# Expert weights split into parts in the front through three buffers, and the last shared outputs stored from ACT's queue

## The chip, the cores and the metric

The kernel runs on one core of one Trainium2 chip. The metric is the device time of one execution in microseconds. In the profile PE is TensorE, PEld its weight loads, DVE is VectorE, ACT ScalarE, POOL GpSimd and SP SyncE; SPq, ACTq and POOLq are the DMA issues of an engine. DVE runs everything that subtracts and adds, ACT what copies, scales or applies a function, SP only issues DMAs and waits.

## The reference

X is (2, 2048, 512) in fp32, so 4096 tokens of width D = 512; H = 256 per expert, E = 8 experts, two for each token.

```python
h = layernorm(layernorm(X)) * ln_w + ln_b
Q, K, V = split(h @ W_in + b_in); Q, K = rope(Q), rope(K)
A = sum over tokens of (K / |K|) * V          # one vector per sequence
x2 = X + layernorm((A * Q) @ W_out + b_out + layernorm(X))
xf = layernorm(x2)
top_logits, idx = top_k(xf @ gate_w, 2); gates = softmax(top_logits)
routed = sum over the two experts of gate * (gelu(xf @ w1[e] + b1[e]) @ w2[e] + b2[e])
shared = gelu(xf @ sw1 + sb1) @ sw2 + sb2
out = x2 + layernorm(routed + shared)
```

## The kernel before

Each fp32 factor is held as a high and a low part, and each product is three matmuls (hi·hi, lo·hi, hi·lo; lines 1434 to 1436). ACT makes the high part by a copy, DVE (in a few places POOL) the low part by a subtraction. Tokens go in NG = 8 groups of G = 512, a group in GT = 4 tiles of 128. Each engine has its own program, and the order in it is written out by hand; semaphores tie them together.

**Front** (span 26 to 316 us). For each group g: K and V products of four tiles (`kv`), the turn of the next group's h (`turn`, eight transposes a bank in two banks of `tp`, for which ACT writes `hb` and the high part in `front_split(g+1)`), then the Q products (`q`). DVE does `k_tile`, `v_tile` and `kv_prod` of a tile, `q_lo_parts(g-1)` after the third tile's K, and `rotate_q(g)`; ACT does `norm_k(g, j)`, the square of a K tile, for which it waits on DVE, and after the fourth `front_split(g+1)` and `bias_q(g)`. SP issues, in this order in each group: `load_x(g+2)`, `store_q(g-1)` (waits for `q_lo_parts(g-1)`), `load_rt(g+1)`, `load_rf(g+1)`, and then, in g = 1 to 4, copies of two experts' `w1` and `w2` from DRAM to `expert_scratch`, laid out anew, and in g = 5 those of `sw1` and `sw2`. The output weights `wo` are scaled by A at the ends of the two sequences, `scale_wo(0)` after group GB = 4.

**Attend** (316 to 570). For group s: `attend(s, j)` is A·Q@W_out plus a rank one product with `bo` (64 rows, of which two hold the parts of b_out; L1509), `z_tile`, `x2_tile`, `norm_x2(s)`; between them the normalised n3 of group s-1 is turned (`n3_turn`) and gated (`gate`). A `fill` slot (s = 2 to 7) puts a half of a shared expert of the groups in EARLY there: "h" (first product, `hs`, gelu, low parts) in one s, "o" (second product, `f_out`, stores of f) in the next. At s = 0 ACT and POOL split the shared weights (`split_s`); load order on SP is q, s. The experts' weights are 64 KB a partition in `we[e]`: parts 2i (high) and 2i+1 (raw, then low). After the last group SP loads raw parts (`load_expert`), ACT makes `split_expert`, DVE `expert_lo`.

**Routing** (566 to 657). `n3_turn(7)`, `shared_o(6, j)`, `gate(7)`, counts and ranks of the experts (`rank_ps`), `shared_h(7, m)`, then 16 blocks of the hot loop (L1601: DVE makes marks `hot_a`, `hot_q` for HT tiles, ACT scales `hot_a`, PE multiplies them into the list of token ids), with `shared_o(7, j)` and `f_out(7, j)` between them; then POOL gathers rows by indirect DMA.

**Expert loop** (657 to 910). NRT = 72 tiles of 128 slots: gather, turn, `h_of`, gelu, `o_of`, gate, and scatter with addition to `f_scratch`, which was zeroed for the groups in LATE and holds the shared outputs for those in EARLY.

**Late** (910 to 1026). For the three groups of LATE: `late_turn` (two banks `tp`, `nc_hi` by ACT, `nc_lo` by DVE), `late_h`, `late_o`; and for all groups `normed`, the layer norm of f, whose result POOL adds to `out` in DRAM by accumulating stores (L1413). Its weights `c1`, `c2` are loaded raw and split there again. `measured` and `normed_in` say after which late product each early tile's moments and norm stand.

Of the kernel before, what the change touches and what calls it, by code (L numbers as in the profile page):

```python
# [7 lines left out]
P = 128  # L8
F32 = mybir.dt.float32
# [4 lines left out]
ALU = mybir.AluOpType  # L14
# [5 lines left out]
EARLY = (1, 3, 5, 6, 7)  # L20


def sandwich_kernel(nc, X, ln_w, ln_b, W_in, b_in, W_out, b_out, gate_w, w1, b1, w2, b2,
# [39 lines left out]
    we_dram = dram("expert_scratch", (E, 2, P, KD * H))  # L63
    ws_dram = dram("shared_scratch", (2, P, KD * SH))
# [9 lines left out]
    with ctx:  # L74
# [23 lines left out]
        upper, ones_f = keep("upper", [P, P]), keep("ones_f", [P, P])  # L98
# [43 lines left out]
        wo_lo = [at("wo_lo0", 136, [P, KD, D], F32R), at("wo_lo1", 8, [P, KD, D], F32R)]  # L142
        rc, rsn = at("rc", 144, [P, 2, G]), at("rsn", 148, [P, 2, G])
# [3 lines left out]
        sq, prod = [at(f"sq{i}", 176 + 2 * i, [P, D]) for i in range(2)], [at(f"prod{i}", 180 + 2 * i, [P, D]) for i in range(2)]  # L147
# [3 lines left out]
        raw_o = [at(f"raw_o{i}", kb_, [P, D]) for i, kb_ in enumerate((194, 196, 198, 110))]  # L151
# [8 lines left out]
        bo_raw, bo_hi = at("bo_raw", 96, [B_ROWS, D]), at("bo_hi", 98, [B_ROWS, D], F32R)  # L160
        bo, bo_one = at("bo", 108, [B_ROWS, D], F32R), at("bo_one", 100, [B_ROWS, P], F32R)
# [11 lines left out]
        zero_d = at("zero_d", 72, [P, D])  # L173
# [32 lines left out]
        c1_hi, c1_lo = at("c1_hi", 96, [P, KD, SH], F32R), at("c1_lo", 104, [P, KD, SH], F32R)  # L206
        c2_hi, c2_lo = at("c2_hi", 112, [P, KS, D], F32R), at("c2_lo", 120, [P, KS, D], F32R)
        c_raw = [at(f"c_raw{i}", kb_, [P, KD, SH]) for i, kb_ in enumerate((136, 164))]
        hsc = [at(f"hsc{i}", 144 + 2 * i, [P, G]) for i in range(2)]
        hc_hi, hc_lo = at("hc_hi", 148, [P, KS, G], F32R), at("hc_lo", 156, [P, KS, G], F32R)  # L210
        fst, fmv = at("fst", 192.125, [P, NT, 6]), at("fmv", 193, [P, NT, 2])
# [7 lines left out]
        rank_ps, ids_ps = bank[2], bank[0]  # L219
        xt_ps, th_ps, h_ps, oe_ps = bank[0:2], (bank[2], bank[7]), bank[3:5], bank[5:7]  # L220
# [9 lines left out]

        fill = {2 + i: (("h", "o")[i % 2], EARLY[i // 2]) for i in range(6)}
        assert all(fill[s][1] == s - 1 for s in (2, 4, 6))
# [8 lines left out]
        h_order = (1, 3, 5, 6, 7)  # L241
# [3 lines left out]
        f_buf = {n: n % 2 for n in range(len(f_order) - GT)}  # L245
        f_buf.update({len(f_order) - GT + j: (2, 3, 4, 0)[j] for j in range(GT)})
        f_buf_uses = [sum(b == u for b in f_buf.values()) for u in range(2)] + [3]

        def f_sem(u):
            return f_stored[min(u, 2)]  # L250
# [14 lines left out]
        measured = beside((0, 0, 0, 0, 1, 1, 1, 1, 2, 2, 2, 2, 1, 1, 0, 0, 2, 2, 1, 1, 0, 0, 0, 0))  # L265
        normed_in = beside((0, 0, 0, 0, 0, 0, 0, 0, 0, 1, 1, 1, 2, 2, 2, 2, 1, 1, 1, 1, 2, 1, 1, 1))
# [16 lines left out]
        f_loads = (EARLY[0], LATE[0], EARLY[1], EARLY[2], LATE[1], EARLY[3], LATE[2], EARLY[4])  # L283


        w_order = (3, 4, 0, 5, 1, 2, 6, 7)

        front_in, consts_in, late_in, rows_in = sem("front_in"), sem("consts_in"), sem("late_in"), sem("rows_in")
# [8 lines left out]
        we_copied, ws_copied = sem("we_copied"), sem("ws_copied")  # L297
# [13 lines left out]
        bo_in, bo_set, bo_hi_done, bo_split = sem("bo_in"), sem("bo_set"), sem("bo_hi_done"), sem("bo_split")  # L311
# [4 lines left out]
        x2_stored, n3_stored, f_stored = [sem(f"x2_stored{i}") for i in range(2)], sem("n3_stored"), [sem(f"f_stored{i}") for i in range(3)]  # L316
# [3 lines left out]
        s_in, s_hi_done, s_split = [sem(f"s_in{i}") for i in range(2)], sem("s_hi_done"), sem("s_split")  # L320
# [6 lines left out]
        we_in, we_hi_done, we_split = [sem(f"we_in{i}") for i in range(E)], sem("we_hi_done"), sem("we_split")  # L327
        bias_in = [sem(f"bias_in{i}") for i in range(2)]
# [9 lines left out]
        c_split = sem("c_split")  # L338
        n3c_in, f_in = [sem(f"n3c_in{i}") for i in range(len(LATE))], [sem(f"f_in{i}") for i in range(NG // 2)]
# [4 lines left out]
        y_normed, stored = sem("y_normed"), sem("stored")  # L344
# [4 lines left out]
        def _(sp):  # L349
# [29 lines left out]
            sp.dma_start(b2_rows[:, :], b2).then_inc(rows_in, 16)  # L379
            sp.dma_start(sb2_rows[:, :], sb2.partition_broadcast(E)).then_inc(rows_in, 16)  # L380
# [3 lines left out]
            for k in range(KD):  # L384
                sp.dma_start(raw_o[k][:, :], W_out[k * P:(k + 1) * P, :]).then_inc(o_raw_in, 16)
# [3 lines left out]
            def copy_expert(e):  # L389
                sp.dma_start(we_dram[e, 0].rearrange("p (k h) -> p k h", k=KD), w1[e].rearrange("(k p) h -> p k h", p=P))\  # L390
                  .then_inc(we_copied, 16)
                sp.dma_start(we_dram[e, 1].rearrange("p (k d) -> p k d", k=KH), w2[e].rearrange("(k p) d -> p k d", p=P))\
                  .then_inc(we_copied, 16)
# [5 lines left out]

            for g in range(NG):  # L400
# [12 lines left out]
                if g == 5:  # L413
                    for i, w in enumerate((sw1, sw2)):
                        sp.dma_start(ws_dram[i].rearrange("p (k h) -> p k h", k=KD), w.rearrange("(k p) h -> p k h", p=P))\
                          .then_inc(ws_copied, 16)
# [6 lines left out]
            def load_s(i, lo):  # L423
                sp.dma_start(lo[:, :, :].rearrange("p k h -> p (k h)").bitcast(F32), ws_dram[i]).then_inc(s_in[i], 16)

            sp.wait_ge(tp_full, KD * NG)
            sp.dma_start(bo_raw[:, :], b_out.partition_broadcast(B_ROWS)).then_inc(bo_in, 16)
# [16 lines left out]
            for s in range(NG):  # L444
# [3 lines left out]
                if s == 2:  # L448
                    sp.wait_ge(consts_set, F_ZERO)
                    for g in LATE:  # L450
                        sp.dma_start(f_groups[g], zero_d[:, :].rearrange("p (o d) -> p o d", o=1).to_broadcast([P, GT, D]))\
                          .then_inc(zero_stored, 16)
                    sp.dma_start(f_dram[N:N + 4 * P, :].rearrange("(t p) d -> p t d", p=P),
                                 zero_d[:, :].rearrange("p (o d) -> p o d", o=1).to_broadcast([P, 4, D])).then_inc(zero_stored, 16)
# [6 lines left out]
                if s + 2 < NG:  # L461
                    load_x(NG + s + 2)
# [1304 lines left out]
```

## Time and profile before

| | us |
|---|---|
| median of 3 runs (lowest, highest) | 1025.62 (1023.91, 1026.31) |
| profiled execution, own time | 1027.98 |
| its span | 1025.8 |
| TensorE busy in the span | 896.8 |
| VectorE busy | 628.3 |
| ScalarE busy | 442.0 |
| GpSimd busy | 404.4 |
| mean granted TensorE clock | 0.95 |

The span is the part that the profiler records; 2.2 us of the execution's own time lie outside it. Busy time is the time in which an engine works on some instruction; waiting for semaphores and issuing DMAs is not in it. The granted clock is 1.00 at TensorE's higher level (2.4 GHz) and 0.50 at its lower one (1.2 GHz); a value between is a mean over a stretch in which both occur. DMA share is the mean busy share of the core's sixteen DMA engines. In a timeline row the bracket at the end is the idle time of the engine before the instruction, and what it had waited for; in the list of waits "times" counts the waits and the last number is the longest.

### The profile page before, as it was taken

Reading aid. Unit: us, or ns where it says so; the run is one execution under the profiler, and the core shown is the slowest. Engines: PE = TensorE matmul, PEld = TensorE weight load, DVE = VectorE, ACT = ScalarE, POOL = GpSimd, SP = SyncE. Lnnn points to the kernel's source line nnn. Section 1 sums busy time; section 2 is a strip of 40 time slices with the busy share of each in tenths; the row PEclk is TensorE's granted clock in tenths of the full one; section 3 lists DMA queues with packets and bytes.
Section 4 is the critical chain, followed back from the end, with each engine's and each line's share of the span. In section 5 each row is a group of like instructions: output and inputs, shape, how many; then the busy total and the mean of one; then the engine's idle time right before and its main releaser. Section 6 shows DMA issues by size and latency. Waiting matters only on the chain.

```text
span 1025.8 us, 14729 instructions
## 1 busy us (share of the span) xinstructions
PE 896.8 (87%) x4562; PEld 739.3 (72%) x4562; DVE 628.3 (61%) x1356; ACT 442.0 (43%) x830; POOL 404.4 (39%) x337
## 2 busy tenths in 40 slices
PE   1999999999997699999999748499999999969883
PEld 1877787787785467777778537488988988857662
DVE  5656766676664775656665587366665666655653
ACT  4134233433423124122242645366666666653462
POOL 3356446545631400000000000277677777730464
PEclk9999999999998889999999878799999999989886
DMA  9122644545337568645424650678778878789496
GB/s 314 45 81 105 244 143 161 188 158 200 135 144 306 190 239 312 227 165 215 154 83 169 215 151 32 238 144 149 140 147 163 154 146 149 147 176 350 62 160 107
DMA packets 78074, 174.68 MB, mean 170 GB/s; under 512 B 10841, under 2 KB 19289, under 8 KB 73137
## 3 DMA queue, kind: packets, MB, share of 16 engines
q1 hardware_dynamic: 52096, 124.60, 33.6%
q0 software_dynamic: 20592, 45.96, 25.1%
q10 hardware_dynamic: 5312, 3.18, 1.3%
q8 instruction: 41, 0.67, 0.3%
q14 instruction: 33, 0.26, 0.1%
HBM read 103.68 MB, written 80.53 MB: 180 GB/s over the span
## 4 chain that ended last, share of the span: by engine, by line
PE 70%; DVE 11%; issue 7%; ACT 4%; POOL 3%; DMA 2%; SPq 1%; POOLq 0%; ACTq 0%; DVEq 0%
PE bank L1434 12%; PE bank L1435 12%; PE bank L1436 12%; PE bank L1626 3%; PE bank L1628 3%; PE bank L1627 3%; PE bank L1643 3%; PE bank L1645 3%; PE bank L1644 3%; PE bank L1613 3%; PE bank L1429 3%; POOL out L1413 2%; DVE we L1061 2%; PE bank L1635 2%; ACT hb L535 1%
## 5 line engine op out<-in xcount | busy, mean ns | idle before, releaser
L1385 POOL DMA_INDIRECT f_scratch<-ro,dst x71 | 113.2, 1595 | 48.7 <-SPq L513 23.2
L1377 POOL DMA_INDIRECT xr<-n_scratch,ids x72 | 71.1, 987 | 90.9 <-issue 65.6
L1434 PE MATMUL bank<-wkv_hi,h_hi 128*128 128x512 f32 x256 | 101.1, 395 | 3.8 <-issue 3.8
L1436 PE MATMUL bank<-wkv_hi,h_lo 128*128 128x512 f32 x256 | 100.7, 393 | 0.0
L1435 PE MATMUL bank<-wkv_lo,h_hi 128*128 128x512 f32 x256 | 100.6, 393 | 0.0
L1188 DVE TENSOR_TENSOR ro<-bank,b2b 128x512 f32<-128x512 f32 x71 | 49.1, 692 | 70.3 <-PE bank L1645 70.3
L1626 PE MATMUL bank<-we,x_hi 128*128 x284 | 86.4, 304 | 0.0
L1628 PE MATMUL bank<-we,x_lo 128*128 x284 | 80.7, 284 | 0.0
L1627 PE MATMUL bank<-we,x_hi 128*128 x284 | 80.6, 284 | 0.0
L544 ACT ACTIVATE sq<-kb 128x512 f32<-128x512 f32 x32 | 20.3, 633 | 134.2 <-DVE kb L845 134.2
L1344 POOL TENSOR_TENSOR zr<-zv,half 128x4 f32<-128x4 f32 x8 | 8.1, 1009 | 137.7 <-DVE zv L961 137.7
L1296 POOL TENSOR_TENSOR rn<-ssq,half 128x1 f32<-128x1 f32 x32 | 23.4, 731 | 96.2 <-ACT sq L544 96.2
L1434 PEld LDWEIGHTS bank<-wkv_hi,h_hi 128*128 128x128 f32 x256 | 48.7, 190 | 14.3 <-issue 4.2
L1643 PE MATMUL bank<-we,g_hi 128*128 x142 | 56.6, 399 | 1.2 <-DVE g_lo L1180 1.2
L1168 DVE TENSOR_TENSOR x_lo<-bank,x_hi 128x512 fp32r<-128x512 f32 x72 | 49.7, 690 | 11.4 <-ACT x_hi L704 9.9
L1645 PE MATMUL bank<-we,g_lo 128*128 x142 | 56.4, 397 | 0.0
L1435 PEld LDWEIGHTS bank<-wkv_lo,h_hi 128*128 128x128 f32 x256 | 48.8, 191 | 10.2
L1644 PE MATMUL bank<-we,g_hi 128*128 x142 | 56.1, 395 | 0.0
L1436 PEld LDWEIGHTS bank<-wkv_hi,h_lo 128*128 128x128 f32 x256 | 48.6, 190 | 10.3
L1626 PEld LDWEIGHTS bank<-we,x_hi 128*128 128x128 f32 x284 | 54.3, 191 | 0.3 <-issue 0.3
L1434 PE MATMUL bank<-wo_hi,q_hi 128*128 128x512 f32 x128 | 54.3, 424 | 0.0
L1627 PEld LDWEIGHTS bank<-we,x_hi 128*128 128x128 f32 x284 | 54.3, 191 | 0.0
(232 smaller groups left out, 2514.2 us busy)
## 6 DMA issues: line engine op xcount, KB each, us to landing
xg<-in_X SPq DMA_DIRECT2D x16, 1024.0 KB, 9.1
q_scratch<-qh SPq DMA_DIRECT2D x8, 1024.0 KB, 3.9
q_scratch<-qb SPq DMA_DIRECT2D x8, 1024.0 KB, 7.1
expert_scratch<-in_w SPq DMA_DIRECT2D x16, 512.0 KB, 7.1
q_hi<-q_scratch SPq DMA_DIRECT2D x8, 1024.0 KB, 4.7
q_lo<-q_scratch SPq DMA_DIRECT2D x8, 1024.0 KB, 6.9
out<-z SPq DMA_DIRECT2D x8, 1024.0 KB, 5.1
n_scratch<-n SPq DMA_DIRECT2D x8, 1024.0 KB, 6.4
```

The source lines that it names most:

```text
L1168: dve.tensor_tensor(x_lo[u][:, :], xt_ps[u][:, :], x_hi[u][:, :].bitcast(F32), ALU.subtract)\
L1377: pool.indirect_dma_start(xr[u][:, :], None, n3_dram, bass.IndirectOffsetOnAxis(ids[:, i:i + 1], 0)).then_inc(row_in[u], 16)
L1385: pool.indirect_dma_start(f_dram, bass.IndirectOffsetOnAxis(dst[:, i:i + 1], 0), ro[i % NRO][:, :], None, compute_op=ALU.add).then_inc(r_s ...
L1434: pe.matmul(dst, hi(k), w_hi(k), start=(k == 0), stop=False)
L1435: pe.matmul(dst, hi(k), w_lo(k), start=False, stop=False)
L1436: last = pe.matmul(dst, lo(k), w_hi(k), start=False, stop=(k == KD - 1 and not more))
L1626: pe.matmul(out_h, x_hi[u][:, s], part_of(e, 0, k, H), start=(k == 0), stop=False)
L1627: pe.matmul(out_h, x_hi[u][:, s], part_of(e, 1, k, H), start=False, stop=False)
L1628: last = pe.matmul(out_h, x_lo[u][:, s], part_of(e, 0, k, H), start=False, stop=(k == KD - 1))
L1643: pe.matmul(oe_ps[u][:, :], g_hi[u][:, s], part_of(e, 2, k, D), start=(k == 0), stop=False)
L1644: pe.matmul(oe_ps[u][:, :], g_hi[u][:, s], part_of(e, 3, k, D), start=False, stop=False)
L1645: last = pe.matmul(oe_ps[u][:, :], g_lo[u][:, s], part_of(e, 2, k, D), start=False, stop=(k == KH - 1))
```

## The change

The order of the groups' shared experts is another one: EARLY is (0, 2, 4, 6, 7), with fill slots s = 1 to 7. Expert and shared weights are no longer copied from DRAM to DRAM and split later. They are 20 units of 512 KB; in each of the groups 1 to 5 four units are loaded to SBUF, split by one ACT copy (`unit_hi`) and one DVE subtraction (`unit_lo`) and stored as two parts, through three pairs of buffers (UB = 3). So `split_s`, `split_expert`, `expert_lo` and the splits of c1 and c2 are gone, and twice as many bytes are loaded for experts (16 MB) and shared weights. The parts of b_out are made in group 0. f of group 6 and 7 is stored from ACT's queue, group 6 through buffers of its own. At s = 7 the DVE does the whole x2 chain at once. Two of the `shared_o(7, j)` come ahead of the hot loop. In the late stage n3 and c1_hi are loaded only after the first eight turns of the expert loop, `late_turn` uses four banks, each f load has its own semaphore, and the last late group is written by plain stores from SP after DVE has added x2.

```diff
-EARLY = (1, 3, 5, 6, 7)
+EARLY = (0, 2, 4, 6, 7)
...
-    we_dram = dram("expert_scratch", (E, 2, P, KD * H))
-    ws_dram = dram("shared_scratch", (2, P, KD * SH))
+    we_dram = dram("expert_scratch", (E, 4, P, KD * H))
+    ws_dram = dram("shared_scratch", (2, 2, P, KD * SH))
...
+        UG = 4
+        units = [(e, i, 0) for e in range(E) for i in range(2)] + [(E + i, 0, h) for i in range(2) for h in range(2)]
+        UB = 3
+        w_lo = [at(f"w_lo{i}", kb_, [P, UW], F32R) for i, kb_ in enumerate((128, 132, 194))]
+        w_hi = [at(f"w_hi{i}", kb_, [P, UW], F32R) for i, kb_ in enumerate((136, 140, 176))]
...
+            def load_unit(u):
+                if u >= len(units):
+                    return
+                if u >= UB:
+                    sp.wait_ge(w_stored[u % UB], 32 * (u // UB))
+                w, k = unit_in(u)
+                sp.dma_start(w_lo[u % UB][:, :].bitcast(F32).rearrange("p (k h) -> p k h", k=k), w).then_inc(raw_w_in[u % UB], 16)
+
+            def store_unit(u):
+                sp.wait_ge(unit_split, u + 1)
+                for c, w in ((0, w_hi), (1, w_lo)):
+                    sp.dma_start(unit_out(u, c), w[u % UB][:, :].bitcast(F32)).then_inc(w_stored[u % UB], 16)
...
             for g in range(NG):
+                u = UG * (g - 1)
+                with_units = 0 <= u < len(units)
                 sp.wait_ge(h_normed, g + 1)
                 load_x(g + 2)
+                if with_units:
+                    store_unit(u)
+                    load_unit(u + 2)
                 if g >= 1:
                     store_q(g - 1)
+                if with_units:
+                    store_unit(u + 1)
+                    load_unit(u + 3)
+                    store_unit(u + 2)
+                    load_unit(u + 4)
                 if g + 1 < NG:
                     sp.wait_ge(k_rotated, GT * (g + 1))
                     load_rt(g + 1)
+                if with_units:
+                    store_unit(u + 3)
+                    load_unit(u + 5)
+                if g + 1 < NG:
                     sp.wait_ge(q_rotated, g + 1)
                     load_rf(g + 1)
-                if 1 <= g <= 4:
-                    copy_expert(2 * g - 2)
-                    copy_expert(2 * g - 1)
...
-            sp.wait_ge(ws_copied, 32)
-            load_s(1, s2_lo)
             store_q(NG - 1)
+            for u in range(UB):
+                sp.wait_ge(w_stored[u], 32 * u_uses[u])
             sp.wait_ge(q_stored[1], 32 * NG // 2)
             load_q(1)
-            load_s(0, s1_lo)
+            load_s(0, (s1_hi, s1_lo))
...
+            def load_expert(e, parts=range(4)):
+                c = slice(parts[0], parts[-1] + 1)
+                sp.dma_start(we[:, e, c, :].bitcast(F32), we_dram[e, c].rearrange("c p h -> p c h")).then_inc(we_in, 16)
...
+            for j in range(GT):
+                sp.wait_ge(y_added, j + 1)
+                sp.dma_start(out_tiles[GT * LATE[2] + j], f[LATE[2]][:, j, :]).then_inc(late_stored, 16)
...
+            def unit_hi(u):
+                act.wait_ge(raw_w_in[u % UB], 16 * (u // UB + 1))
+                if u >= UB:
+                    act.wait_ge(w_stored[u % UB], 32 * (u // UB))
+                act.activation(w_hi[u % UB][:, :], w_lo[u % UB][:, :].bitcast(F32), ACT.Copy).then_inc(unit_hi_done, 1)
...
                     if j == 1 and g >= 1:
                         q_hi_parts(g - 1)
+                    if 0 <= UG * (g - 1) < len(units):
+                        unit_hi(UG * (g - 1) + j)
                 if g + 1 < NG:
                     front_split(g + 1, (g + 1) % 2)
...
-            act.wait_ge(bo_in, 16)
-            act.activation(bo_hi[:, :], bo_raw[:, :], ACT.Copy).then_inc(bo_hi_done, 1)
-            act.wait_ge(bo_set, 1)
-            act.activation(bo[0:1, :], bo_raw[0:1, :], ACT.Copy).then_inc(bo_split, 1)
...
             for m in range(KS):
                 gelu(7, m)
-            split_expert(2)
+                store_f(6, m)
...
             for k in range(KD):
                 act.wait_ge(tc_full, KD * i + k + 1)
-                act.activation(nc_hi[:, k, :], tp[k % 2][:, :], ACT.Copy).then_inc(nc_hi_done, 1)
+                act.activation(nc_hi[:, k, :], tc[k][:, :], ACT.Copy).then_inc(nc_hi_done, 1)
...
                 kv_prod(g, 0)
+                unit_lo(g, 0)
...
                     q_lo_parts(g - 1)
+                unit_lo(g, 1)
...
                 kv_prod(g, 2)
+                unit_lo(g, 2)
                 v_tile(g, 3)
                 kv_prod(g, 3)
+                unit_lo(g, 3)
                 rotate_q(g)
...
-            expert_lo((5, 1, 2, 6))
...
-                if b in (4, 7, 10, 13):
-                    f_out(7, (b - 4) // 3)
-                if b == 9:
-                    expert_lo((7,))
+                for j in {2: (0, 1), 5: (2,), 8: (3,)}.get(b, ()):
+                    f_out(7, j)
...
             for s in range(NG):
                 z_rsqrt(s)
-                if s == 0:
-                    split_s(1, s2_hi, s2_lo)
                 x2_rsqrt(s)
-                if s == 0:
-                    split_s(0, s1_hi, s1_lo)
```

## Rows read from the trace of the kernel before

**Rows 1.** The page's engine totals: busy us, share of the span, instructions.
```profile
PE 896.8 (87%) x4562; PEld 739.3 (72%) x4562; DVE 628.3 (61%) x1356; ACT 442.0 (43%) x830; POOL 404.4 (39%) x337
```

**Rows 2.** Windows by stage: stretch, length, busy us of PE, PEld, DVE, ACT, POOL; clock, DMA share, GB/s.
```profile
100.00:200.00 100.00, 96.51 (x445) 78.99 (x444) 69.09 (x140) 33.90 (x59) 49.06 (x38) 1.00 0.53 188
600.00:640.00 40.00, 22.39 (x106) 18.89 (x104) 33.44 (x60) 22.52 (x66) 0.00 (x0) 0.74 0.28 74
900.00:940.00 40.00, 30.31 (x147) 24.59 (x146) 18.61 (x27) 19.51 (x32) 8.49 (x5) 0.87 0.90 266
980.00:1026.00 46.00, 24.45 (x93) 18.90 (x91) 17.37 (x55) 18.48 (x27) 24.17 (x29) 0.76 0.85 136
```

**Rows 3.** TensorE's waits over the span: us in total, times, longest.
```profile
PE bank L1601 <- ACT hot_a L698: 19.6, 4, 15.5
PE bank L1429 <- DVE n_lo L991: 15.3, 8, 7.2
...
PE bank L1429 <- ACT hb L535: 12.6, 16, 4.3
PE bank L1613 <- DMA xr<-n_scratch,ids: 10.4, 2, 5.9
PE bank L1429 <- DVE nc_lo L1211: 10.4, 3, 4.4
PE bank L1429 <- ACT n L628: 9.9, 1, 9.9
PE bank L1509 <- DVE bo L935: 6.7, 1, 6.7
```

**Rows 4.** Timeline of the front's group 2: start, us, engine, line, operation.
```profile
100.86 0.39 PE L1434 MATMUL bank<-wkv_hi,h_hi 128*128 128x512 f32 x1
...
114.73 0.69 DVE L836 TENSOR_TENSOR kb<-bank,bkv 128x512 f32<-128x512 f32 x1 [0.34 <-PE bank L1436]
...
117.33 2.35 DVE L877 TENSOR_TENSOR qb<-qb,qh 128x1024 f32<-128x1024 f32 x2
...
123.26 0.78 ACT L535 ACTIVATE hb<-bank,lnb,lnw 128x512 f32<-128x512 f32 x1 [0.30 <-PE bank L1429]
...
137.06 0.39 PE L1434 MATMUL bank<-wkv_hi,h_hi 128*128 128x512 f32 x1
```

**Rows 5.** Groups by shape of the experts' splits: busy us, mean ns, idle before.
```profile
L674 ACT ACTIVATE we<-we 128x1024 fp32r<-128x1024 f32 x16 | 15.6, 1043 | 1.5 <-DVE picked L1127 1.5
...
L1061 DVE TENSOR_TENSOR we<-we 128x1024 fp32r<-128x1024 f32 x16 | 18.5, 1219 | 0.0
```

**Rows 6.** Windows: a stretch of the front, and the start of attend.
```profile
120.00:125.00 5.00, 4.32 (x25) 3.32 (x23) 4.83 (x9) 2.37 (x5) 2.62 (x3) 1.00 0.94 367
...
326.00:331.50 5.50, 5.50 (x12) 4.01 (x13) 1.54 (x3) 0.23 (x1) 0.00 (x0) 0.50 0.79 301
```

**Rows 7.** DMA issues from 100 to 137 us: KB each, us to landing.
```profile
q_scratch<-qb SPq DMA_DIRECT2D x1, 1024.0 KB, 7.1
rf<-in_rope_feat SPq DMA_DIRECT2D x1, 512.0 KB, 4.2
```

**Rows 8.** Timeline at the start of attend, and z of the next group.
```profile
326.41 0.43 SPq L420 DMA_DIRECT2D q_lo<-q_scratch  x1
...
342.35 4.73 POOL L1355 TENSOR_TENSOR s_lo<-s_lo,s_hi 128x1024 fp32r<-128x1024 f32 x2
...
344.68 3.61 DVE L967 SCALAR_TENSOR_TENSOR z<-z,zr,xg 128x512 f32<-128x512 f32 x2
...
371.19 1.41 DVE L967 SCALAR_TENSOR_TENSOR z<-z,zr,xg 128x512 f32<-128x512 f32 x2
```

**Rows 9.** The page's DMA issues over the span: KB each, us to landing.
```profile
q_lo<-q_scratch SPq DMA_DIRECT2D x8, 1024.0 KB, 6.9
```

**Rows 10.** Timeline of the routing, DVE.
```profile
591.85 0.69 DVE L1023 COPY fo<-bank 128x512 f32<-128x512 f32 x1 [2.52 <-DMA f_scratch<-fo]
```

**Rows 11.** Timeline of the end, POOL's last stores.
```profile
1011.18 4.44 POOL L1413 DMA_DIRECT2D out<-f  x5
```

More of the change, by code:

```diff
@@ L142, in sandwich_kernel @@
         wo_lo = [at("wo_lo0", 136, [P, KD, D], F32R), at("wo_lo1", 8, [P, KD, D], F32R)]
+        UW = KD * H
+        UG = 4
[3 more added lines that the diff above has]
+        w_hi = [at(f"w_hi{i}", kb_, [P, UW], F32R) for i, kb_ in enumerate((136, 140, 176))]
+        u_uses = [len(range(i, len(units), UB)) for i in range(UB)]
         rc, rsn = at("rc", 144, [P, 2, G]), at("rsn", 148, [P, 2, G])
@@ L599, in _ @@
                     keep_acol(0)
+                if g == GB + 2:
+                    for u in range(UB):
+                        act.wait_ge(w_stored[u], 32 * u_uses[u])
                     scale_wo(0)
@@ L629, in norm_x2 @@
                                    scale=xr_[:, j:j + 1]).then_inc(n3_ready, 1)
-            def split_s(i, hi, lo):
-                act.wait_ge(s_in[i], 16)
-                for h in range(2):
-                    s = slice(2 * h, 2 * h + 2)
-                    act.activation(hi[:, s, :], lo[:, s, :].bitcast(F32), ACT.Copy).then_inc(s_hi_done, 1)
             def gelu(g, m):
@@ L782, in _ @@
                     gelu_c(i, m)
-                for g, j in y_of[what, i, m]:
-                    normed(g, j)
                 if what == "h" and m == KS - 1 and i + 1 < len(LATE):
@@ L787, in _ @@
                         nc_hi_part(i + 1, k)
+                for g, j in y_of[what, i, m]:
+                    normed(g, j)
             normed(*y_order[-1])
@@ L877, in q_lo_parts, with unit_lo @@
                     dve.tensor_tensor(q[:, s, :], q[:, s, :], qh[:, s, :].bitcast(F32), ALU.subtract).then_inc(q_split, 1)
+            def unit_lo(g, j):
+                u = UG * (g - 1) + j
+                if 0 <= u < len(units):
+                    dve.wait_ge(unit_hi_done, u + 1)
+                    dve.tensor_tensor(w_lo[u % UB][:, :], w_lo[u % UB][:, :].bitcast(F32), w_hi[u % UB][:, :].bitcast(F32), ALU.subtract)\
+                       .then_inc(unit_split, 1)
             def wo_lo_parts(b):
-                if b == 0:
-                    dve.wait_ge(b2_stored, 16)
                 for k in range(KD):
@@ L1055, in _ @@
             s = NG - 1
-            def expert_lo(es):
-                for e in es:
-                    for i in range(2):
-                        dve.wait_ge(we_hi_done, 2 * w_order.index(e) + i + 1)
-                        lo = we[:, e, 2 * i + 1, :]
-                        dve.tensor_tensor(lo, lo.bitcast(F32), we[:, e, 2 * i, :].bitcast(F32), ALU.subtract)\
-                           .then_inc(we_split, 1)
-            for m in range(KS):
+            x2_tile(s, 0)
+            x2_tile(s, 1)
+            x2_stats(s, 0)
+            x2_tile(s, 2)
+            x2_stats(s, 1)
+            x2_tile(s, 3)
+            x2_stats(s, 2)
+            x2_stats(s, 3)
+            x2_moments(s)
+            hs_lo_part(6, 0)
+            x2_shift(s)
+            for m in range(1, KS):
                 hs_lo_part(6, m)
+            top2(s - 1)
             dve.memset(zero_q[:, :].bitcast(F32), 0.0)
@@ L1085, in _ @@
             f_out(6, 3)
-            expert_lo((0,))
             dve.wait_ge(counts_full, 1)
@@ L1370, in _ @@
             pool.wait_ge(gates_stored, 16)
-            for u in range(3):
+            pool.wait_ge(zero_stored, 16 * (len(LATE) + 1))
+            for u in range(4):
                 pool.wait_ge(f_stored[u], 16 * f_buf_uses[u])
@@ L1576, in _ @@
                     part(g, i)
-            for m in range(KS):
-                shared_h(6, m)
             n3_turn(NG - 1)
@@ L1590, in _ @@
             pe.matmul(rank_ps[:, 0:E * NT], upper[:, :], marks, start=True, stop=True)
-            pe.matmul(rank_ps[:, E * NT:2 * E * NT], ones_f[:, :], marks, start=True, stop=True).then_inc(counts_full, 1)
+            pe.matmul(rank_ps[:, E * NT:2 * E * NT], ones_f[:, :].bitcast(F32), marks, start=True, stop=True).then_inc(counts_full, 1)
             for m in range(KS):
                 shared_h(7, m)
+            shared_o(7, 0)
+            shared_o(7, 1)
             pe.wait_ge(consts_set, ZEROS_SET)
```

303 lines of the change are left out of this document (156 added, 147 removed).

## Prediction

> **What bounds the kernel now.** I read the engines' totals first: TensorE is busy 87% of the span, every other engine under two thirds [rows 1]. So time is gained or lost where TensorE stands idle or runs at its lower clock, and the windows by stage say where that is. In the front the reader is to see 96.5 us of matmuls in 100 at granted clock 1.00; the ends are elsewhere: in the routing 22 us of 40 at 0.74, at the end of the expert loop 30 of 40 at 0.87, in the last 46 us 24 [rows 2]. The list of TensorE's waits names what it stood for [rows 3]: the marks (19.6 us), `n_lo` (15.3), `nc_lo` (10.4), the first gathers (10.4), n of group 0 (9.9), `bo` (6.7). Of `hb`, the front's own input, it waits only 12.6 us in 16 times: this list is also a list of what has cover and can lose it. Last come the timelines around each edit.
>
> **The front, g = 1..5: the loss.** Call T the start of a group's K products (100.86); the next group's is 36.2 us on [rows 4]. ACT has nothing to do from the last `norm_k` until the banks of the next turn are full, and starts `front_split` at 123.26, T+22.4; TensorE needs it at once (the following turn, then the Q products). The change puts `unit_hi(4g-1)` in that place, and it waits for a DMA. When does that DMA land? SP issues it behind `store_q(g-1)` and `store_unit(4g-3)`. `store_q` waits for `q_lo_parts`, which ends at 119.68, T+18.8. One `unit_lo` is put ahead of it on the DVE, one behind it: 1.22 each [rows 5], of which the DVE's idle 0.34 at 114.73 takes some, so `store_q` is issued at T+19.7. In front of the unit's last byte there are then 2 MiB of Q, 1 MiB of the unit's parts and its own 0.5: 3.67 MB. At the 367 GB/s from 120 to 125 [rows 6] 10.0 us; the row of `q_scratch<-qb` (2 MiB, landed 7.1 us after its issue, of which 5.7 are bytes [rows 7]) adds 1.4, and the issues 0.4. It lands at T+31.5, and ACT's copy, 1.04 [rows 5], ends at T+32.6. That is 10.2 after `front_split` starts now, and TensorE stands for it. Behind the waiting copy on ACT are `front_split` and `bias_q`; on SP, `store_unit(4g-1)` waits for the same unit, and `load_rf(g+1)` behind it has a whole group of time. A stall also lowers the clock: after the 6.7 us wait for `bo` the window from 326 to 331.5 shows 0.50, the lower of its two levels [rows 6], which costs 2.7. I take 2.2 us here, since the first microsecond is transposes that ACT paces anyway. 12.4 a group, five groups: **62**.
> Bounds. If the load doesn't queue behind the stores, it is issued at T+22.2 and lands in the 4.2 us of `rf` (512 KB) [rows 7]: stall 5.0, clock 1.5, together 32.5. If the DMA is in time, ACT's 1.04 and the DVE's added copies ahead of the last K tiles (4 × 1.22 a group, the DVE at 69% [rows 2]) leave about 3.3 a group, 16.5. If the queue is a tenth slower, 68. I take the queue, because the row of `rf` itself (4.2 for 1.4 us of bytes) and `qb` both show landings that grow with what was issued before.
> The Trainium skill (DMA: Bandwidth & Descriptors, section "Anatomy of one DMA — SWDGE (gpsimd) path") gives about 2.0 us fixed and 436 GB/s for a transfer; its fit is for transfers issued by GpSimd, so for these it is an estimate. By it the 3.67 MB would take 10.4 us instead of the rows' 11.4, and the sum would be 5 us lower, 1026; the rows' rate is used.
> The `bo` parts in g = 0 cost ACT 0.3 there, and the stores of `f(0,*)`, now behind the zero fills, about 1.0. Loss **63.3**.
> Covered: the loads' bytes themselves (the queues are at 0.53 in the front [rows 2]), POOL in the front (49%), SP's waits, since nothing SP holds back but `rf` and `rt` is needed within a group.
>
> **Start of attend: a gain.** `bo` is ready long before: 6.7 of wait [rows 3] and 2.7 of half clock go. The wait for n of group 0, 9.9 [rows 3], goes too: POOL's `s_lo` splits, 4.73 for two [rows 8], stretch the DVE's instructions beside them (z for two tiles 3.61, later 1.41 [rows 8]) and delay the chain z, x2, n. Against it `load_q(1)`, issued at 326.41 [rows 8], lands at 333.3 (6.9 us, [rows 9]), when TensorE is ready for it at 329.7: 3.3 for it and 1.0 of clock. Sum **15.0**; bounds 9 (the chain stays) to 19 (no new wait).
>
> **Routing: a gain.** `n_lo` of the last group waits 7.2 [rows 3]; with x2's chain ahead of everything at s = 7 I work out 4.0, so 3.3, and 1.4 earlier in that chain. `f_out(6,*)` gets own buffers, and the 2.52 wait for a store [rows 10] and 0.8 behind it go: 3.3. `expert_lo(5,1,2,6)`, eight of 1.15, 9.2 [rows 5], stands between the gates and the marks, for which TensorE waits; 2.5 come back as waits for `hs`: 6.7. In the hot loop `expert_lo(7)` goes, 2.4, and 1.6 of waits for banks: 4.0. Gathers of the first rows wait behind two other loads; of the 10.4 [rows 3] go 4.1. Less 1.3 for clock. Sum **21.5**, bounds 14 to 27. The cover that this needs: 16 MB of expert parts instead of 8. Counted from the stage in which they start, they and the biases land 8 to 10 us before the expert loop asks.
>
> **Late: a gain.** With four banks and n3 in time the waits for `nc_lo` go, 10.4 [rows 3], and the clock of 0.87 over 40 us [rows 2], 5.2, with it: 16 with what remains of `hc_lo`. After the last matmul five accumulating stores follow one another from POOL, 4.44 for the issue alone [rows 11], to the end at 1025.8; one plain store a tile from SP behind one DVE add saves 5.5 (bounds 2 to 8). **21.5**, bounds 15 to 25.
>
> **Sum.** Gains 15.0 + 21.5 + 21.5 = 58.0, losses 63.3: +5.3. The profiled execution took 1027.98 us (span 1025.8), so 1033.3 for it; the median of the three runs shown is 1025.62, 2.4 below, so **1031**. The two sides are of one size, each with some 8 us of doubt: the sign hangs on the front. Break-even is a loss of 11.3 a group, a landing at T+30.4.
>
> **Rivals.**
> *A, the unit's load passes the stores* (other side). If the sixteen engines serve a later read beside queued writes, the stall is 5.0 and a group loses 6.5: losses 33.8, gains 58.0, **1001**. For it: `rf` landed after 4.2 us. Against it: it was issued when the Q stores had nearly drained. It decides from a landing before T+30.4.
> *B, the expert parts become the wait.* They, b1 and b2, 17.8 MB, take 48.5 us at 367 GB/s; at the 266 GB/s of a shared stretch [rows 2] 67, and 18.5 less the 8 of slack and with the clock after a stall is about 12 more: **1043**. For it: gathers, zero fills and stores of x2 and f share these queues. Against it: the routing's share is 0.28 [rows 2].
> *C, the units are in time*, and only ACT's and DVE's instructions count: losses 17.8, **985**. It needs `store_q` out of the way, for which no row speaks.
>
> **How the numbers follow.** Forecast (values 1020 to 1042) 0.50; A 0.27; B 0.14; C 0.09. Within 0.2% (2 us, what a measurement here can tell from no change) of 1025.62 lies 0.08 of the forecast, faster 0.08, slower 0.34. Faster: 0.08 + 0.27 + 0.09 = 0.44; same 0.08; slower 0.34 + 0.14 = 0.48. The range reaches down into A, whose own values are 996 to 1008, and up over B's middle: 997 to 1048, and leaves out C and the edges. The likeliest case's own range is 1020 to 1042.
>
> **What would show it.** Right: in five groups TensorE waits about 10 us in the turn's transposes on ACT `hb`, ACT being idle before a copy `w_hi<-w_lo` that a DMA releases, at a distance from K products to K products of 48.6, not 36.2; no wait on `bo`; a wait of 3 us for `q_hi` or `q_lo`; the marks' wait under 8; no wait of note for `nc_lo`; 10 us from the last matmul to the end instead of 17. Wrong: a distance of 42.7 (A) or 39.5 (C); the first expert matmul waiting for `we` (B). The forecast falls if the loads land before T+30, or if any of the three gains is under its lower bound.

## The result and the profile after

The changed kernel took 1050.27 us (1046.55 to 1053.11, 4 runs) beside 1024.88 for the kernel before: ratio 1.0244, 95% interval 1.0208 to 1.0281. That is 25 us slower, where 5 us slower was forecast, and 2 us above the top of the range. Its profiled execution took 1049.15 us, span 1047.4, so 21.6 more than the span before. The kernel before took 1025.6 us on one chip and 1030.1 on another (medians), so below a run is compared by its ratio to the kernel before on the same chip, or inside one trace.

Stage by stage, from the first and last start of a group of instructions in the two traces (us from the span's start):

| TensorE at | before | after | difference |
|---|---|---|---|
| last K product of the front | 303.9 | 359.5 | +55.6 |
| first turn of n (group 0) | 359.0 | 402.0 | +43.0 |
| last turn of n (group 7) | 575.6 | 618.9 | +43.3 |
| DVE's first marks of the hot loop | 615.8 | 649.0 | +33.2 |
| last matmul of the hot loop | 644.3 | 682.6 | +38.3 |
| first product of the expert loop | 657.3 | 691.7 | +34.4 |
| first late turn | 911.0 | 947.6 | +36.6 |
| last matmul of all | 1008.2 | 1039.0 | +30.8 |
| end of the span | 1025.8 | 1047.4 | +21.6 |

The loss is in the front, and it never comes back in full. TensorE's waits after, which answer to [rows 3] (us in total, times, longest):

```profile
PE bank L1481 <- ACT hb L598: 58.0, 16, 10.3
...
PE bank L1481 <- DVE n_lo L1046: 10.6, 8, 2.0
PE bank L1655 <- ACT hot_a L751: 9.4, 6, 6.4
PE bank L1667 <- DMA xr<-n_scratch,ids: 5.9, 2, 5.7
PE bank L1481 <- DMA n3c<-n_scratch: 4.8, 1, 4.8
PE bank L1486 <- DVE hc_lo L1276: 4.4, 2, 2.2
...
PE bank L1486 <- DMA q_lo<-q_scratch: 3.8, 1, 3.8
PE bank L1486 <- DVE fo L1080: 3.6, 1, 3.6
...
PE bank L1740 <- DMA c_lo<-shared_scratch: 1.9, 1, 1.9
```

`bo` and `nc_lo` are gone; `hb` has risen from 12.6 to 58.0. The 9.9 us wait for n of group 0 is gone too: its turn, at 401.98, has no wait ahead of it. The 1.5 us that the list still has for `ACT n` stand in the last group:

```profile
612.64 0.66 PE L1481 MATMUL bank<-ident,n 128*128 128x128 f32 x4 [1.55 <-ACT n L702]
```

The timeline of one front group, which answers to [rows 4], shows how:

```profile
111.09 0.39 PE L1486 MATMUL bank<-wkv_hi,h_hi 128*128 128x512 f32 x1
...
130.65 0.32 SPq L426 DMA_DIRECT2D q_scratch<-qh  x1
...
134.53 1.24 SPq L416 DMA_DIRECT2D w_lo<-in_w  x1
...
142.30 1.06 ACT L647 ACTIVATE w_hi<-w_lo 128x1024 fp32r<-128x1024 f32 x1 [6.17 <-DMA w_lo<-in_w]
143.26 0.76 ACT L598 ACTIVATE hb<-bank,lnb,lnw 128x512 f32<-128x512 f32 x1
...
144.07 1.12 PE L1481 MATMUL bank<-ident,hn 128*128 128x128 f32 x4 [10.18 <-ACT hb L598]
...
158.65 0.39 PE L1486 MATMUL bank<-wkv_hi,h_hi 128*128 128x512 f32 x1
```

Read from T = 111.09: Q's stores at T+19.6, the fourth unit's load at T+23.4, its copy at T+31.2, TensorE idle for 10.18 us, and the next group 47.6 us on instead of 36.2.

In the hot loop a new row stands on ACT's queue. Its second number is the time of the issue itself:

```profile
656.99 0.36 ACT L751 ACTIVATE hot_a<-hot_a,token 128x72 fp32r<-128x72 f32 x1 [3.87 <-DVE hot_q L1201]
657.00 7.58 ACTq L740 DMA_DIRECT2D f_scratch<-fo  x1
...
665.11 0.60 ACT L751 ACTIVATE hot_a<-hot_a,token 128x72 fp32r<-128x72 f32 x2 [7.02 <-issue]
```

ACT can't scale the next marks while it stands in that issue, and TensorE waits 6.39 us for them. And near the start of the late stage the windows show TensorE idle for 9 us in 30, with the queues full (length, busy us of PE, PEld, DVE, ACT, POOL, clock, DMA share, GB/s):

```profile
950.00:980.00 30.00, 21.22 (x89) 17.48 (x90) 12.76 (x28) 8.61 (x14) 2.74 (x3) 0.89 0.95 327
980.00:1010.00 30.00, 27.82 (x130) 22.74 (x129) 24.88 (x73) 16.28 (x25) 15.28 (x19) 1.00 0.96 258
```

The kernel before has the same picture in the first 30 us of its late stage, but its queues are emptier behind them, at 136 GB/s:

```profile
910.00:940.00 30.00, 21.60 (x92) 17.44 (x93) 13.26 (x17) 14.12 (x21) 4.60 (x3) 0.83 1.00 329
940.00:970.00 30.00, 25.60 (x111) 21.23 (x110) 22.39 (x63) 14.00 (x21) 11.12 (x13) 0.89 0.62 136
```

### The profile page after: what moved, and what is told of

It is laid out like the page before. It is cut to its first block, busy times and chain, and to the rows that moved or that the text cites. A ratio compares the mean times of both kernels' runs of the same rounds, so it can differ in the third digit from the quotient of the medians.

```text
span 1047.4 us, 14773 instructions
## 1 busy us (share of the span) xinstructions
PE 905.8 (86%) x4562; PEld 746.4 (71%) x4562; DVE 627.1 (60%) x1359; ACT 438.8 (42%) x826; POOL 399.6 (38%) x329
## 4 chain that ended last, share of the span: by engine, by line
PE 60%; DVE 16%; DMA 10%; ACT 6%; issue 5%; SPq 2%; POOL 1%; DVEq 0%; POOLq 0%; ACTq 0%
PE bank L1486 10%; PE bank L1487 9%; PE bank L1488 9%; PE bank L1680 3%; PE bank L1681 3%; PE bank L1682 3%; PE bank L1697 3%; PE bank L1699 3%; PE bank L1698 3%; DMA w_lo<-in_w 3%; PE bank L1667 3%; DMA f_scratch<-ro,dst 2%; PE bank L1481 2%; DVE w_lo L929 2%; PE bank L1689 1%
## 5 line engine op out<-in xcount | busy, mean ns | idle before, releaser
L1481 PE MATMUL bank<-ident,hn 128*128 128x128 f32 x128 | 25.2, 345 | 71.1 <-ACT hb L598 58.0
L1481 PEld LDWEIGHTS bank<-ident,hn 128*128 128x128 f32 x128 | 18.4, 175 | 76.9 <-ACT hb L598 62.9
L1356 POOL TENSOR_TENSOR rn<-ssq,half 128x1 f32<-128x1 f32 x32 | 27.5, 860 | 106.5 <-ACT sq L607 106.5
L1486 PEld LDWEIGHTS bank<-wkv_hi,h_hi 128*128 128x128 f32 x256 | 48.6, 190 | 14.3 <-issue 4.2
L1487 PEld LDWEIGHTS bank<-wkv_lo,h_hi 128*128 128x128 f32 x256 | 48.6, 190 | 10.2
L1488 PEld LDWEIGHTS bank<-wkv_hi,h_lo 128*128 128x128 f32 x256 | 48.6, 190 | 10.2
L702 ACT ACTIVATE n<-z,xnm,xr__76 128x512 f32<-128x512 f32 x32 | 23.5, 805 | 77.2 <-DVE xnm L1039 77.2
```

What stands on the lines that cost most here:

```text
L1481: last = pe.transpose(dst[:, j * P:(j + 1) * P], src[:, j, k * P:(k + 1) * P], ident[:, :])
L1486: pe.matmul(dst, hi(k), w_hi(k), start=(k == 0), stop=False)
L1487: pe.matmul(dst, hi(k), w_lo(k), start=False, stop=False)
L1488: last = pe.matmul(dst, lo(k), w_hi(k), start=False, stop=(k == KD - 1 and not more))
```

## The experiments

Each is an edit of the changed kernel unless it says otherwise.

**The fourth unit off the front's path.**

```diff
-                    if 0 <= UG * (g - 1) < len(units):
+                    if 0 <= UG * (g - 1) < len(units) and j < GT - 1:
                         unit_hi(UG * (g - 1) + j)
                 if g + 1 < NG:
                     front_split(g + 1, (g + 1) % 2)
                     bias_q(g)
+                if 0 <= UG * (g - 1) < len(units):
+                    unit_hi(UG * (g - 1) + GT - 1)
...
-                unit_lo(g, 3)
                 rotate_q(g)
                 if g + 2 < NG:
                     front_stats(g + 2)
+                unit_lo(g, 3)
```

> The changed kernel with the fourth unit of each group taken off the front's path: its ACT copy stands behind front_split and bias_q, its DVE subtraction behind rotate_q. Theory (the fourth unit's load, queued behind the stores, holds ACT and so the turn): the distance from K products to K products falls from 47.6 us to 36.5 to 38.5, TensorE's wait on hb from 58.0 us to under 16, and the time from 1050 to about 1003 (995 to 1012). Rival (the added DVE copies, four of 1.22 us a group, or the doubled bytes bound the group): the distance stays above 42 and the time above 1025.

Ratio 0.9883 (0.9859 to 0.9906): 3.5% less than the changed kernel, some 37 us, and now faster than the kernel before. On the scale of the kernel before, 1025.6 us, that is 1014, just above the expected 995 to 1012. The wait on `hb` is 24.0, not under 16. The copies of the fourth unit, which now stand behind `bias_q`, are 40.0 us apart (105.46, 145.42, 185.46), and so are the starts of the K products (104.68, 144.63, 184.67). The unit was two thirds of the front's loss. The distance is between theory and rival: 3.8 us a group are left, and they are something else.

**Q's stores behind the fourth unit's load.**

```diff
-                if g >= 1:
-                    store_q(g - 1)
                 if with_units:
                     store_unit(u + 1)
                     load_unit(u + 3)
+                if g >= 1:
+                    store_q(g - 1)
+                if with_units:
                     store_unit(u + 2)
```

> The changed kernel with one thing moved on SP: store_unit of the second unit and the load of the fourth are issued ahead of store_q. Theory (the load lands late because 2 MiB of Q stores are ahead of it in the queue): the fourth unit lands 5 to 6 us earlier, the ACT wait before its copy falls from 6.2 us by as much or to nothing, the wait on hb by 25 to 30 us in all, and the time to 1020 to 1026. Rival (the queues serve the read beside the stores, and it is late for its own issue time, or for the third unit's sake): the landing moves by less than 2 us and the time stays within 8 us of 1050.

Ratio 1.0096 (1.0079 to 1.0113), 1.4% less, some 15 us, little over half of what was expected; the wait on `hb` falls by 14 (to 44.0), not by 25 to 30. The rows of the fourth unit's load and copy, and of the stores ahead of them:

```profile
130.87 0.32 SPq L421 DMA_DIRECT2D expert_scratch<-w_hi  x1
...
131.71 0.78 SPq L416 DMA_DIRECT2D w_lo<-in_w  x1
...
137.32 1.06 ACT L648 ACTIVATE w_hi<-w_lo 128x1024 fp32r<-128x1024 f32 x1 [3.20 <-DMA w_lo<-in_w]
```

From the first store in the way to the copy it is 6.45 us, where the changed kernel needs 11.65 (130.65 to 142.30): 5.2 less for 2 MiB less, as a queue at 367 to 400 GB/s would have it (5.7 to 5.2). Counted from its own issue, the load lands after 5.6 us instead of 7.7. But the stores start 2.2 us later in the group, since they wait for the second unit's subtraction, which stands behind Q's on DVE, so the copy comes only 3.0 us earlier (28.2 us into it instead of 31.2) and the group shortens from 47.6 to 44.4. The read does queue behind the writes; the expectation had left DVE's order out.

**Where ACT's 7.6 us come from.** Two runs: the stores of f(7,*) from SP, and the store of the gates from SP.

```diff
-            act.dma_start(gates_out, picked[:, :, :]).then_inc(gates_stored, 16)
...
+            sp.wait_ge(gates_ready, 1)
+            sp.dma_start(gates_out, picked[:, :, :]).then_inc(gates_stored, 16)
             sp.wait_ge(o_full, NO)
```

> The changed kernel with the four stores of f(7,*) issued by SP, behind b1 and ahead of b2, instead of by ACT inside the hot loop. Theory (ACT stands 7.6 us in the issue of one store, and the marks behind it on ACT are late): TensorE's wait of 6.4 us for hot_a goes, with some half clock; the time falls by 6 to 9 us, to 1041 to 1044. Rival (the hot loop is bound by DVE or by TensorE, which only catch up): the time stays within 2 us.

> The changed kernel with the store of the gates (4096 pieces of 8 bytes) issued by SP behind b1 instead of by ACT; the stores of f(7,*) stay on ACT. It tells apart why ACT's issue of the first f(7,*) store took 7.6 us. Theory (ACT's own queue is full of the gates' pieces): the issue takes 0.3 to 0.4 us, the 6.4 us wait for hot_a goes and the time falls by 5 to 9 us. Rival (the sixteen engines are busy with the last expert's parts and b1, whatever the queue): the issue still takes over 5 us and the time stays within 2 us.

Ratios 1.0182 (1.0164 to 1.0201) and 1.0118 (1.0088 to 1.0147), 0.6% and 1.2% less: some 6 and 13 us. The second is more than the 5 to 9 expected; its trace has 9.5 of it by the first product of the expert loop (682.2 instead of 691.7), and the rest is within the two intervals. With the stores of f(7,*) on SP and the gates still on ACT, TensorE's wait for `hot_a` falls from 9.4 to 2.2, and none of the four stores takes SP more than 0.33 us to issue. With the gates on SP the same store, at the same place and beside the same loads, is issued at once:

```profile
656.53 0.35 ACT L751 ACTIVATE hot_a<-hot_a,token 128x72 fp32r<-128x72 f32 x1 [3.82 <-DVE hot_q L1201]
656.54 0.33 ACTq L742 DMA_DIRECT2D f_scratch<-fo  x1
...
663.17 4.05 SPq L549 DMA_DIRECT2D b2b<-b_scratch  x1
```

The slow issue has moved with the gates: the load of b2, the next on SP's queue behind them, takes 4.05 us to issue there and 0.33 in the changed kernel, but nothing in the hot loop waits for SP.

The hot loop's matmuls take 18.3 us from first to last (654.7 to 673.0) instead of 27.4. So it was what ACT's own queue held: in the changed kernel the gates, issued at 649.10 as 4096 pieces of 8 bytes, took 20.4 us to land (9.0 before), and the next issue on that queue waited. It did not wait for all of them: it ended at 664.58, they landed at 669.5, and the two issues in between took 0.44 and 0.33 us. The busy engines alone didn't do it; how much they added by making the gates slow to land was not tried.

**n3 of the late groups from ACT's queue.** The two loads were moved behind c1_lo and c2_lo in `act.dma_start`.

> The changed kernel with n3 of the second and third late group loaded from ACT's queue, where c1_lo, c2_hi and c2_lo are issued, instead of from SP behind the landing of the last scatters. Theory (the late stage lost its gain to loads that start late): TensorE's wait of 4.8 us for n3c and the half clock behind it (0.74 from 970 to 980) go, the wait for the second part of c1 stays near 1.9, and the time falls by 5 to 8 us. Rival (the queue is full in this stretch, 330 to 390 GB/s from 955 to 990, so that what comes earlier pushes f or c2 later): a wait for c2 or f takes its place and the time stays within 3 us.

Ratio 1.0258 (1.0211 to 1.0305): no gain, and the rival's picture. The wait for n3c is gone, and these stand in its place (the releaser isn't resolved; at 970.78 it is the first product that reads c2, whose parts landed 14.9 and 16.4 us after their issue):

```profile
951.96 0.76 PE L1736 MATMUL bank<-nc_hi,c_hi 128*128 128x512 f32 x1 [4.51 <-issue]
970.78 0.76 PE L1487 MATMUL bank<-c_hi,hc_hi 128*128 128x512 f32 x1 [4.33 <-issue]
```

The first of the two is ACT's: with five issues (945.40 to 948.70) ahead of `nc_hi` its copies begin 3.2 us behind the first turn (948.74 and 945.5), where the changed kernel needs 1.3.

**Half the shared weights' bytes.** On top of that, the late groups' products take c1_hi and c2_hi in place of the low parts, which aren't loaded.

> The changed kernel with n3 of the late groups from ACT's queue, and without the loads of c1_lo and c2_lo: the late stage's products take c1_hi and c2_hi in their place, so the same matmuls run, with 2 MiB less to load (the low parts of the shared weights are left out of the late groups' result). Theory (the late stage's missing gain lies in its loads, twice the bytes of before for the shared weights, in a queue that runs full at 387 GB/s): 2 MiB are 5.4 us; the waits ahead of the first second product (4.3) and of the second parts go, and the late stage from its first turn to its last matmul shrinks from 93 us by 5 to 9. Rival (hc_lo, the clock and the norm chain bound it): by less than 3 us.

From the first late turn to the last matmul the late stage takes 85.4 us (950.9 to 1036.3), where it took 93.2 (945.5 to 1038.7) in the run before this and 91.4 in the changed kernel. That is 7.8 us less, inside the theory's 5 to 9, but not all of it is bytes: with three issues instead of five ahead of `nc_hi` on ACT, its copies begin 1.4 us behind the first turn instead of 3.2. Some 6 us are left for the 2 MiB, which is also the difference to the changed kernel. The wait ahead of the second product is 0.88:

```profile
970.87 0.47 PE L1486 MATMUL bank<-c_hi,hc_hi 128*128 128x512 f32 x1 [0.88 <-issue]
```

The ratio, 1.0224 (1.0201 to 1.0246), moved less, by 0.3%, within both intervals, so the gain is seen in the stage and not shown in the time. In this trace the expert loop, whose code is the same, was 4.6 us longer than in that of the run before (253.3 us against 248.7 from first to last turn).

**Accumulating stores again.** The last late group as before: no load of x2, no `add_x2`, POOL accumulates.

> The changed kernel with the last late group written as before: no load of x2, no DVE addition, accumulating stores from POOL. Theory (the accumulating stores, one behind the other, were what the end cost): from the last matmul to the end of the span 8.4 us become 15 to 17.5, and the time is 6 to 9 us longer. Rival (without x2's 1 MiB and the DVE additions the late stage itself is shorter by as much): the time stays within 3 us.

Ratio 1.0306 (1.0282 to 1.0329), 0.6% or 6 us more. From the last matmul (1043.9) to the end (1057.6) it is 13.7 us, where the changed kernel needs 8.0 and the kernel before 17.2, so less than the 15 to 17.5 expected. The plain stores are worth 5.7 of the 9.2; that the norms are spread differently over the late stage is likely the rest, but no run had that alone.

**The kernel before with bo early alone.** Its parts made in group 0, as in the change.

> The kernel before with one part of the change alone: the two parts of b_out are made in group 0. Theory of the prediction: the 6.7 us wait and 2.7 us of half clock go, 3.3 us of wait for the Q parts and 1.0 of clock come, 0.3 is lost in group 0, and the 9.9 us wait for n of group 0 stays: 5 us less, ratio 0.995. Rival (the shared weights, split by POOL and ACT at their own times, hold the chain to n of group 0 where it is, so its wait grows by what bo's lost): ratio 0.999 to 1.001.

Ratio 0.9933 (0.9913 to 0.9952), 7 us less, more than the 5 expected. The first turn of n comes at 348.9 instead of 359.0:

```profile
332.63 0.50 PE L1433 MATMUL bank<-wo_hi,q_hi 128*128 128x512 f32 x1 [3.60 <-DMA q_lo<-q_scratch]
348.93 1.97 PE L1428 MATMUL bank<-ident,n 128*128 128x128 f32 x8 [4.53 <-ACT n L628]
```

The new wait for Q is there with nearly the forecast's size (3.6 for 3.3), and 5.3 us of the 9.9 for n of group 0 went without POOL's splits being touched.

**Putting it together.** Three moves (unit, gates, n3), two moves (unit, gates), and two orders of DVE's subtractions.

> The changed kernel with three moves together: the fourth unit off the front's path, the gates stored from SP, n3 of the late groups from ACT's queue. If they are independent, the ratios multiply: 1.0244 less 3.6% for the unit (measured alone), less 1.0% for the gates (alone), less 0.6% for n3: about 0.975 of the kernel before. If the gains hide each other: above 0.983.

Ratio 0.9806 (0.9774 to 0.9838): between the two figures.

> The changed kernel with two moves: the fourth unit off the front's path and the gates stored from SP; n3 of the late groups stays on SP. By the two measured alone the ratio would be 0.9883 x 1.0118 / 1.0244 = 0.976. If loading n3 from ACT's queue was worth nothing or less, this is as fast as the run with three moves (0.981) or faster; if it was worth something after all, 0.985 or more.

Ratio 0.9788 (0.9768 to 0.9807). n3 from ACT's queue is worth nothing that these runs can tell, as when it was tried alone.

> As the run with the three moves together, but the front's units in another order: three of a group's four DVE subtractions stand behind the last kv_prod, where DVE waits for the Q products (6.9 us idle), only the first stays ahead of the K tiles, SP stores the three together and then loads the next three, and the fourth unit's ACT copy stands between front_split and bias_q. Theory (what is left of the front's loss after the fourth unit is moved, 3.8 us a group, is the three DVE subtractions, 4.8 us, ahead of the last K tile): the distance from K products to K products falls from 40.0 to 37 to 38 us and the time by 10 to 15 us more, to a ratio of 0.962 to 0.968. Rival (what is left is DMA landing and the doubled traffic): the distance stays at 39.5 or more and the ratio at that of the three moves.

Ratio 0.9877 (0.9847 to 0.9907), 0.7% slower than the three moves, and the distance is 41.2 us (109.38, 150.71, 191.84). The theory fell in this form. (The execution in the trace took 1005.83 us where the median is 1012.17, so it shows only part of the loss.) DVE's subtractions now lie beside POOL's low parts of h, and ACT waits for those:

```profile
128.79 3.44 DVE L929 TENSOR_TENSOR w_lo<-w_lo,w_hi 128x1024 fp32r<-128x1024 f32 x2
...
131.11 3.53 POOL L1351 TENSOR_TENSOR h_lo<-hb,h_hi 128x512 fp32r<-128x512 f32 x2
...
133.47 0.78 ACT L595 ACTIVATE hb<-bank,lnb,lnw 128x512 f32<-128x512 f32 x1 [4.30 <-POOL h_lo L1351]
...
137.82 0.79 PE L1486 MATMUL bank<-h_hi,wq_hi 128*128 128x512 f32 x1 [3.14 <-ACT qb L613]
```

Two subtractions take 3.44 us instead of 2.44, POOL's pair 3.53, and the turn's third bank comes late; the fourth unit's ACT copy then stands ahead of `bias_q`, and TensorE waits 3.14 us for a bank.

The last run starts from the two moves again:

```diff
                     q_lo_parts(g - 1)
-                unit_lo(g, 1)
                 v_tile(g, 2)
                 k_tile(g, 3)
+                unit_lo(g, 1)
                 kv_prod(g, 2)
                 unit_lo(g, 2)
```

> The two moves, and the DVE subtraction of the group's second unit moved from ahead of the last K tile to just behind it. It tells what the 3.8 us a group are that the front still loses (distance 40.0 instead of 36.2). Theory (DVE's subtractions ahead of the last K tile, 2.3 us of them this one): the distance falls by 1.5 to 2.3 us, the time by 7 to 11. Rival (as in the run with all three behind it, they then lie beside POOL's low parts of h, which ACT and the turn wait for): the distance stays within 0.7 us and the time within 4 us.

Ratio 0.9711 (0.9685 to 0.9736), 0.8% less than the two moves, 7 to 8 us. The distance, here by ACT's copies of the fourth units, falls from 40.5 (104.55, 144.69, 185.56) to 38.4:

```profile
103.65 1.05 ACT L649 ACTIVATE w_hi<-w_lo 128x1024 fp32r<-128x1024 f32 x1
...
142.00 1.05 ACT L649 ACTIVATE w_hi<-w_lo 128x1024 fp32r<-128x1024 f32 x1
...
180.40 1.05 ACT L649 ACTIVATE w_hi<-w_lo 128x1024 fp32r<-128x1024 f32 x1
```

One move of one instruction. At its old place it stood beside POOL's `accumulate`, and took 2.31 us (the run with two moves):

```profile
122.54 1.90 POOL L1365 TENSOR_TENSOR acc<-acc,prod 128x512 f32<-128x512 f32 x1
...
123.21 2.31 DVE L931 TENSOR_TENSOR w_lo<-w_lo,w_hi 128x1024 fp32r<-128x1024 f32 x1
```

POOL's instruction ends at 124.44, DVE's 1.08 later at 125.52: nearly its whole 1.22 lies behind POOL's. That fits a rule of the Trainium skill (SBUF — State Buffer, section "SBUF: two separate sides"): a DVE instruction with two inputs in SBUF and one of GpSimd's that reads SBUF exclude each other for the whole instruction, they don't share. In the same group the first unit's subtraction starts ahead of POOL's `accumulate` (116.62 and 116.78), and there it is POOL's that is longer, 2.21 instead of 1.27, and DVE's takes 1.22. At its new place it starts behind POOL's `accumulate`, which ends at 123.55, and takes 1.22:

```profile
121.64 1.91 POOL L1365 TENSOR_TENSOR acc<-acc,prod 128x512 f32<-128x512 f32 x1
...
124.83 1.22 DVE L931 TENSOR_TENSOR w_lo<-w_lo,w_hi 128x1024 fp32r<-128x1024 f32 x1
```

This kernel beats both: 2.9% under the kernel before, 5.2% under the changed one.

## Why the prediction was wrong

**The front, 62 forecast.** Right in mechanism and nearly in size. Q's stores at T+19.7 forecast and T+19.6 seen, the copy at T+31.5 and T+31.2, TensorE's stall 10.2 and 10.18, the group 48.6 and 47.6. What comes on top of the stall was taken too dear: 2.2 forecast for the clock, 1.2 by the distances (47.6 less 36.2 and 10.18); that is 5 of the 8 us by which the loss fell short. The clock did fall, for about as long as behind bo's wait (5.5 us [rows 6]):

```profile
144.00:149.00 5.00, 4.65 (x15) 3.68 (x16) 0.61 (x1) 4.67 (x8) 3.83 (x3) 0.50 1.07 395
```

But ACT is busy for 4.67 of these 5 us with the turn that TensorE follows, so part of the half clock costs nothing; that is read from the window, and no run tried it. Rival A (the load passes the stores) is refuted, by the landing itself (T+31.2, where it needed less than T+30.4) and by the run with Q's stores behind it. From the first store's issue to the copy it took 11.65 us; the rows' rate gives 11.8 (11.4 and 0.4 of issues). The estimate from the fixed time and rate of the Trainium skill (DMA: Bandwidth & Descriptors, section "Anatomy of one DMA — SWDGE (gpsimd) path"), 10.4 us or 10.8 with the issues, would have been too short. Rival C's 3.3 a group, ACT and DVE alone, is close to the 3.8 measured once the unit was off the path, and the last run shows that DVE's order is 2.1 of it.

**The start of attend, 15.0.** 12.7 measured (by the unrounded starts) between the last K product and the first turn of n. The new wait for Q came (3.8 for 3.3). The cause named for the 9.9 us wait was half right at most: the run with bo early alone takes 5.3 of it away with POOL's splits in place. What remained, 4.5, is gone in the changed kernel; that POOL's splits held it was not tried alone.

**Routing, 21.5: the step that failed most.** Between the first turn of n and the first product of the expert loop only 8.6 were gained, and 6.4 counted to the first late turn, where the lower bound was 14. Term by term:
- the 3.3 and 1.4 for `n_lo` of the last group came (15.3 to 10.6 in the list, the longest from 7.2 to 2.0), but nothing of them is left by the last turn of n. Two other waits stand beside it there (1.55 and 1.41; no run says why), and `f_out(0,2)` at s = 2 costs 3.6, where 1.0 was allowed for the zero fills: SP stood until 447.78 in their issue before it reached the store, for which DVE then waited. No run moved those fills.
- to the first marks of the hot loop 10.1 were gained (43.3 to 33.2), as `f_out`'s 3.3 and `expert_lo`'s 6.7 add up; no run had the two apart.
- the hot loop, 4.0 forecast, lost 5.1 (33.2 to 38.3). The forecast has no term for the stores of f from ACT's queue, so it put them at nothing, and named no work that hides them. The queue held 4096 small pieces; the issue behind them stopped ACT for 7.6 us, and TensorE waits for what ACT scales in that loop. With the gates elsewhere the loop is 9.1 us shorter, and from the first marks to its last matmul it takes 24.4 us (648.6 to 673.0) against 28.5 in the kernel before: the 4.0 of the forecast. So what failed here is that one term, the store's issue.
- the gathers gained 3.9 for 4.1. Rival B did not happen: no wait on the expert parts is in the list.

**Late, 21.5.** 15.0 came: 5.8 where 16 was forecast, 9.2 where 5.5 was. The waits for `nc_lo` went as forecast, 10.4, and others came: 4.8 for n3, 1.9 for c1_lo, 1.1 more ahead of the first product (2.6 for 1.5), 0.9 more for `hc_lo` (4.4 for 3.5). The step said that the waits go "with four banks and n3 in time"; n3 was not in time, and when it was made so, c2 was late instead. The sum had counted the splits that went and not that twice the bytes come in their place, into queues that [rows 2] show at 266 GB/s over 900 to 940. In the first 30 us of the late stage they ran at 329 GB/s already and run at 327 now; it is behind them that 136 has become 258. With half the bytes the stage is some 6 us shorter, though the time does not show it clear of noise. At the end the plain stores gave 5.7, so the forecast's 5.5 was right; the other 3.5 have no run.

So the sum was off by -15 in routing, -10 in late and -2 in attend, against +8 in the front and +4 at the end. The largest single wrong term is the issue of a store on ACT's queue, costed at nothing, and a run shows it: 9.1 us. The doubled loads of the late stage and the fills ahead of f's store were costed at nothing or too low as well, as the traces show; what took the rest of the gain ahead of the last turn of n stays open.

## What to carry to other kernels

When parts are stored instead of made, the arithmetic that goes is easy to see, and the bytes that come are not: follow each load to its queue, to what is ahead of it, and to the engine that stands in order behind its wait. A DMA moved to a compute engine's queue costs that engine the issue, and the issue can be long when the queue still holds many pieces (7.58 us here, and 0.33 without them); list what that queue was given last. Keep work that waits on a DMA behind the engine's work that TensorE is waiting for; here moving two instructions turned a 2.4% loss into a gain, and a third, moved by one tile, gave 0.8% more.

## What was not expected of the hardware

The issue of a 256 KB store on ACT's queue took 7.58 us when a store of 32 KB in 4096 pieces had been given to the same queue 8 us before, and 0.33 us when those pieces went through SP's. SP pays as well: with the gates on its queue, its next issue took 4.05 us. A DVE subtraction of 128x1024 took 1.22 us by itself and up to 2.32 beside POOL; a pair of POOL's took 2.54 us and 3.53 beside DVE. And the expert loop, with the same code, took 248.7 to 255.7 us from first to last turn over the profiled executions of these kernels, so a single trace can't price a change elsewhere to better than a few us; ratios over several runs can.
